# Second mix of the full layers on four column tiles of 32 columns, and VectorE's shrinkage in whole pieces

## The reference

```
xs = rfft2(x)                              # per channel, 64 x 33 frequencies, complex
h  = relu(complex_linear(xs, w1) + b1)     # per block of 48 channels, 8 blocks
y  = complex_linear(h, w2) + b2
y  = softshrink(y, 0.01)                   # v - min(max(v, -0.01), 0.01), real and imaginary part
x  = irfft2(y) + x
```

## Time and profile before

| | us |
|---|---|
| Median of 3 runs | 2082.43 (2081.65 to 2084.39) |
| The profiled execution | 2080.81 |
| Its span | 2079.0 |
| TensorE busy | 1934.2 (93%) |
| TensorE's weight loads busy | 1581.3 (76%) |
| VectorE busy | 1175.1 (57%) |
| ScalarE busy | 1011.0 (49%) |
| POOL busy | 434.7 (21%) |
| Mean share of full clock on TensorE | 0.976 |

### The profile page before, as it was taken

How to read it: one execution, slowest core, us unless ns; L and a number is a source line. 1 busy time by engine, 2 the same in 40 slices (tenths; PEclk the granted TensorE clock), 3 DMA queues, 4 the chain that set the end, 5 groups by cost and what they waited for, 6 DMA issues and landing times.

```text
span 2079.0 us, 68971 instructions
## 1 busy us (share of the span) xinstructions
PE 1934.2 (93%) x31104; PEld 1581.3 (76%) x31104; DVE 1175.1 (57%) x2480; ACT 1011.0 (49%) x1644; POOL 434.7 (21%) x425
## 2 busy tenths in 40 slices
PE   5999995698998999999999999999899999999997
PEld 4777672576776999999999999999677777777774
DVE  3687887987855433333333333332467667666675
ACT  3766545576753333333333333333466556655652
POOL 3212103975721000000000000000321121211200
PEclk9999996799998999999999999999999999999998
DMA  9424728307444111111111111114813555457214
GB/s 169 92 49 84 128 58 140 59 8 125 117 103 98 31 31 31 31 30 30 30 30 30 30 30 30 30 31 73 130 16 68 91 101 103 70 86 127 60 36 95
DMA packets 299701, 141.05 MB, mean 68 GB/s; under 512 B 275760, under 2 KB 298032, under 8 KB 299440
## 3 DMA queue, kind: packets, MB, share of 16 engines
q1 hardware_dynamic: 299440, 137.08, 35.9%
HBM read 74.14 MB, written 62.91 MB: 66 GB/s over the span
## 4 chain that ended last, share of the span: by engine, by line
PE 81%; DVE 9%; ACT 3%; issue 2%; POOL 2%; DMA 2%; SPq 1%; DVEq 0%; POOLq 0%; ACTq 0%
PE ps L690 19%; PE ps L675 19%; PE ps L523 9%; PE ps L586 8%; PE ps L537 8%; PE ps L602 7%; PE ps L555 5%; PE ps L504 4%; DVE u L934 3%; DVE st L971 2%; PE ps L565 1%; DVE xs L959 1%; PE ps L660 1%; ACT zf L749 1%; POOL xs L1180 1%
## 5 line engine op out<-in xcount | busy, mean ns | idle before, releaser
L1083 DVE TENSOR_TENSOR gl<-g,gh 128x512 fp32r<-128x512 f32 x192 | 156.8, 817 | 476.4 <-ACT gh L869 476.4
L934 DVE TENSOR_TENSOR u<-ps,clamp 64x192 f32<-64x192 f32 (+1 forms) x864 | 377.0, 436 | 27.7
L866 ACT ACTIVATE g<-ps,colp 128x512 f32<-128x512 f32 x192 | 132.3, 689 | 529.4 <-PE ps L675 529.4
L523 PEld LDWEIGHTS ps<-const,z 128*48 128x48 f32 x8384 | 266.6, 124 | 117.2 <-issue 107.2
L729 ACT ACTIVATE z<-ps 64x512 f32<-64x512 f32 x366 | 234.6, 641 | 113.4 <-PE ps L504 106.6
L523 PE MATMUL ps<-const,z 128*48 128x64 f32 (+1 forms) x8384 | 271.5, 217 | 14.0 <-issue 9.0
L1170 POOL COPY xn<-xs 128x512 f32<-128x512 f32 x144 | 151.2, 1088 | 552.7 <-PE ps L504 364.3
L690 PE MATMUL ps<-w2h,gh 128*128 128x384 f32 x768 | 261.8, 341 | 0.0
L690 PE MATMUL ps<-w2h,gl 128*128 128x384 f32 x768 | 258.5, 337 | 0.0
L690 PE MATMUL ps<-w2l,gh 128*128 128x384 f32 x768 | 257.5, 335 | 0.0
L537 PE MATMUL ps<-zf,w 112*64 112x512 f32 (+2 forms) x992 | 248.3, 574 | 5.9 <-ACT zf L749 1.3
(11 more groups left out here) (70 smaller groups left out, 2516.2 us busy)
## 6 DMA issues: line engine op xcount, KB each, us to landing
after<-xs SPq DMA_DIRECT2D x96, 384.0 KB, 5.4
xs<-after SPq DMA_DIRECT2D x94, 384.0 KB, 8.9
after<-om SPq DMA_DIRECT2D x32, 384.0 KB, 4.3
out<-xs SPq DMA_DIRECT2D x32, 384.0 KB, 5.4
xm<-after SPq DMA_DIRECT2D x30, 384.0 KB, 6.3
xs<-in_x SPq DMA_DIRECT2D x24, 384.0 KB, 8.4
wstage<-in_spectral SPq DMA_DIRECT2D x16, 210.0 KB, 5.7
xs<-in_x SPq DMA_DIRECT2D x4, 768.0 KB, 11.9
```

Source lines behind the costliest of these rows:

```text
L523: mm = pe.matmul(ps[a * SIDE:a * SIDE + BLOCK, F2_BANK, n * L.kh:(n + 1) * L.kh], z[:, g % 2, slot, :], basis(col + a * SIDE, L.kh), start ...
L934: dve.tensor_tensor(u[to, g % 2, :, start + b:start + size:BATCH], whole, limited, ALU.subtract).then_inc(u_ready, 1)
L1083: dve.tensor_tensor(gl[:, n % 4, :], g[:, n % 2, :], gh[:, n % 4, :], ALU.subtract).then_inc(g_low, 1)
```

## The change

Two things, and the count of semaphore steps that goes with them. m2 in the full layers makes four matmuls per slot instead of one: for each part a (real, imaginary) and each half k of the 64 frequencies, a stationary operand of 32 columns of h and a moving operand of the 48 weight columns of that part. The output goes to the 32 partitions from a * 64 + k, and all slots of both images lie next to each other, 48 columns each. So the four matmuls of a slot lie on four column tiles of 32 columns, and PSUM holds the part by halves of the partitions, as u does. A group of eight slots takes 384 of the bank's columns, as before.

VectorE limits the whole group as before, and subtracts in one piece of 128 partitions by 384 elements (288 for six slots) straight into u. `u_ready` is counted once per group.

```diff
-        self.spread = 2 * BATCH if self.full else BATCH
+        self.spread = 1 if self.full else BATCH
...
                     for c in range(size):
-                        p, b = c // BATCH, c % BATCH
                         col = READY_SECOND if start + c < SPAN else MINUS
-                        mm = pe.matmul(ps[b * SIDE:(b + 1) * SIDE, bank, p * PAIR:(p + 1) * PAIR],
-                                       h[0:ROWS, n % 2, c * SIDE:(c + 1) * SIDE],
-                                       mix[0:ROWS, g % 2, col:col + PAIR], start=True, stop=True)
+                        for a in range(2):
+                            for k in (0, HALF):
+                                mm = pe.matmul(ps[a * SIDE + k:a * SIDE + k + HALF, bank, c * BLOCK:(c + 1) * BLOCK],
+                                               h[0:ROWS, n % 2, c * SIDE + k:c * SIDE + k + HALF],
+                                               mix[0:ROWS, g % 2, col + a * BLOCK:col + (a + 1) * BLOCK],
+                                               start=True, stop=True)
                     mm.then_inc(m2_done, 1)
...
-                    pairs = size // BATCH
-                    part, data = clamp[:, 0:pairs * PAIR], ps[:, bank, 0:pairs * PAIR]
+                    part, data = clamp[:, 0:size * BLOCK], ps[:, bank, 0:size * BLOCK]
...
-                    for b, a in ((0, 0), (0, 1), (1, 1), (1, 0)):
-                        mine, to = slice(b * SIDE, (b + 1) * SIDE), slice(a * SIDE, (a + 1) * SIDE)
-                        whole, limited = (d[mine].rearrange("p (s a c) -> p a c s", a=2, c=BLOCK)[:, a]
-                                          for d in (data, part))
-                        dve.tensor_tensor(u[to, g % 2, :, start + b:start + size:BATCH], whole, limited,
-                                          ALU.subtract).then_inc(u_ready, 1)
+                    whole, limited = (d.rearrange("p (s c) -> p c s", c=BLOCK) for d in (data, part))
+                    dve.tensor_tensor(u[:, g % 2, :, start:start + size], whole, limited,
+                                      ALU.subtract).then_inc(u_ready, 1)
```

## The result

The changed kernel takes 2206.3 us, median of 4 runs (2205.3 to 2209.0), against 2082.0 us before (4 runs): ratio 1.060, 95% interval 1.058 to 1.0625, 124 us slower. The forecast was 2148 us, its range ended at 2186.

What follows compares the result with a forecast made beforehand. TensorE, busy 93% of the span, was taken to bound the kernel. 2080.8 us +19 (array) +63 (tile shape) +8 (instructions) -14 (hidden) -10 (VectorE) gave 2147, as a median 2148 us; range 2080 to 2186, its own 2120 to 2175.

Steps and rivals of the forecast that it cites:

- What bounds the kernel: Full layers: TensorE has no hole in the steady step, so sparing VectorE is worth little and TensorE's added cost counts fully.
- The array's time: Second mix on TensorE: four smaller matmuls raise a slot from 83 to 95 ns, 19 us over 1584 slots, bounds 0 and 54.
- the fit: Second mix: 1.67 ns per moving column and some 8 ns, giving 88 ns per slot with 48 columns.
- the choice: Second mix: the 95 ns per slot taken between bounds 83 and 117.
- the second rival: Second mix: L504's pace is a floor for records, 117 ns per slot, +54 instead of +19 us; 2183 us; 14%.
- the fourth: Second mix: only two of four column tiles run at once, 166 ns per slot, +131 us; 2260 us; 6%.
- The change of tile shape: Borders of the second mix on TensorE: 0.155 us for each of 408 changes between column tiles of 64 and 32, 63 us.
- 14 hidden: Steps of six slots without L586: a longer second mix fills TensorE's wait for ScalarE's copy, hiding 48 x 0.3 = 14 us.
- Instructions: TensorE's queue: 74 more instruction packets make its stops grow in proportion, 8 us, bounds 0 and 20.
- 10 us forecast: VectorE's one-piece subtraction: shorter TensorE waits in layer 0 and the last stretch, and shorter tails, save 10 us, bounds 5 and 14.
- The third rival: L602's waits in layer 0 and the stages' drains: VectorE's relief outweighs, -14 +0 to +5, 2070 us; 10%.

Runs made afterwards that it cites:

- e6: The changed kernel with VectorE's subtraction in four pieces of 64 partitions instead of one, so the change on TensorE alone; 2204.9 us.
- e2: The kernel before with two matmuls per slot, 32 wide stationary and all 96 moving columns, on four column tiles of 32; VectorE unchanged; 2133.0 us.
- e1: The changed kernel with two matmuls per slot instead of four, 64 wide stationary and 48 moving columns; 2119.1 us.
- e3: The kernel before with VectorE's subtraction in one piece of 128 partitions, TensorE unchanged, output not the reference's; 2058.5 us.

## Why the prediction was wrong

**What bounds the kernel: right.** TensorE does, and what VectorE is spared brings nothing once TensorE is slower (e6).

**The array's time: right in the fit, high in the choice.** 64 records start 0.68 us apart from first to last, 87 ns per slot; the fit had 88, the choice 95. L504's pace of 14.6 ns per record is no floor: these come at 10.8. By that the second rival and the fourth are out: four column tiles do run side by side. The term is 6 us, not 19.

**The change of tile shape: right.** 0.28 us per group of eight in e2 against 0.31, and a time 55 us above before, of which stops and half clock (+8 and half of +17) are some 16: about 40 us against 63 less 14 hidden. The steady groups give the same by count: 144 groups of eight at 0.28 and 72 of six at 0.05 us, less 0.10 for each of the 24 that followed L504 anyway, 42 us. So the rule of the Trainium skill, "TensorEngine Tiling (Array Packing)", Key Properties, is borne out for a split of the width as for one of the height.

**Instructions: this step failed.** "If the stops grow with the packets it is 74/170 of 18 us, 8 us; bounds 0 and 20". The stops grew by 68 us. They don't grow in proportion to the packets but with how far the demand lies over what arrives: e1 and e2 add 25 packets and 8 to 10 us, the next 49 packets add 60. A warning stood in the trace of before: in layers 2 and 3, 105 packets in 595 us, one per 5.7 us; with half again as many instructions in nearly the same time, one per 4 on average and less in the dense steps; and packets never follow each other closer than 3.3 us. So did the other half, that all stops of these layers fell on packets with data in flight. What was read was only the count and the sum of the stops in the second stretch; over the whole span there were 34.8 us, and the spectral stages had some 210 packets, not 170.

**The clock: missing.** No term stood for it. 38 us more at 1.2 GHz are up to 19 us.

**VectorE: too small alone, too large behind the change.** 10 us forecast; 20 us when nothing else changes (e3), 0 with the rest (e6). The third rival's price was 14; it would have decided only if the second mix had cost nothing. Waits of TensorE for VectorE gave 7.5 and 1.0 us, but L602 waited for L959 for 19.4 us in the whole span, 10.8 of them between 330 and 640 us, which the prediction did not look at. In e3 these waits are 10.7 us, TensorE's waits of all kinds 12.5 us fewer, and time at half clock 8 us less, worth up to 4. What gave the last few of the 20 us is not shown; the steady L537 and L602 take 0.86 and 0.65 us in both.

In sum: 40 (shape) + 6 (array) + 68 (stops) + up to 19 (clock) - 0 to 10 = 123 to 133 us for 124 measured. The parts overlap at the clock, and no run separates the clock from the stops.

## What to carry to other kernels

Before splitting matmuls into smaller ones, divide instructions by time, weight loads included, in the densest stretch of a few microseconds, and set it against the closest spacing of instruction packets that the trace has (here 256 instructions per 3.3 to 3.6 us). Then look at the stretches with data transfers in flight by themselves: there packets came 5.2 us apart (median), and even the kernel before, with one per 5.7 us on average, lost 15 us. The average rate is no safe line. Relief of an engine and a load on another don't add: measure the relief by itself (20 us here) before paying for it on the engine that bounds.

## What the runs showed of the hardware

- The supply of instructions to TensorE, above; the Trainium skill, "Runtime: NRT & Kernel Launch", Instruction fetch mechanics, has the blocks of 16 KiB and 256 instructions, which the trace confirms (257 per packet), and says that the fetch stays hidden because instructions are dispatched more slowly than they come in. Here it does not: 64 records and 64 weight loads start within 0.82 us, 6.4 ns each, and 103 us are lost waiting, in layers 2 and 3 mostly (47.6 of 52.0 us) on packets that had data transfers in flight.
- Four column tiles of 32 over 113 rows run side by side in float32: 43 ns per wave of four records with 48 columns.
- Matmul records follow each other at 10.8 ns over a whole group, far below the 25 ns that the prediction cited from the Trainium skill, "TensorE: Matmul & The Clock Gate", Wait — 56ns, not 53.3ns?. They lie on four column tiles; one tile's own records are 43 ns apart.
- The change between column tiles of 64 and 32 costs 0.10 us before it, and some 0.17 us in and behind the group.
